# The relation products of a pair in one run at the head of an iteration

## The chip, the cores and the metric

The kernel runs on one core of a Trainium2 chip. The metric is the device time of one execution in microseconds (us). TensorE is called PE, VectorE DVE, ScalarE ACT, GpSimd POOL and SyncE SP, as in the profile.

## The reference

A graph of 6250 nodes with 256 features and 100000 edges passes through two layers, each a graph step and a feed-forward step with a layer norm ahead and a residual sum behind. Cut to the part in which the change lies:

```python
# layer 0, graph: attention over the incoming edges of each node, 8 heads of 32
e = leaky_relu(a_src[src] + a_dst[dst], 0.2)
alpha = softmax of e over the edges with one dst
x = x + relu(segment_sum(h[src] * alpha, dst) + bias)
# layer 0, feed-forward: one of 32 experts for each node, 64 hidden units
xf = layernorm(x)
idx = argmax(xf @ router_w.T + router_b)
x = x + relu(relu(xf @ W1[idx] + b1[idx]) @ W2[idx] + b2[idx])
# layer 1, graph: 16 relations
transformed = einsum('ni,rio->rno', layernorm(x), weight)
x = x + segment_sum(transformed[edge_type, src] * edge_weight, dst)
# layer 1, feed-forward: 8 experts mixed by two weights, not touched here
```

## The kernel before, in words

The nodes are sorted by their number of incoming edges, most first, and stand in 49 tiles of 128. After a preparation (to about 360 us) the function `attention` computes the attention, the first feed-forward step and `transformed` in one software pipeline (to about 2240 us). `relations` then gathers rows of `transformed`, and the last feed-forward step ends the kernel.

`attention` works on pairs of tiles, g = 0 to 23, and a last single tile, g = 24. Each engine runs its own in-order program, a loop over `pair`, and waits on semaphores of the others. The stages of a pair are spread over several iterations:

- POOL (`tile`, L819) gathers for each edge slot of a tile one row of `h_table` per node, 32 columns at most. A tile's first 16 columns may come once the tile two before it is summed, the others once the tile before it is summed.
- DVE (`tile`) scores the gathered rows (L1201 to L1206), looks up the next indices (L1209 to L1218), waits for ACT's exponential (semaphore `p_ready`), weighs (L1231) and adds (L1240) the rows slot by slot, a tile of high degree having more slots, sums (L1254, L1255) and normalises (L1298 to L1307). In the first tile of pair i, between scores and weighing, stands `lagged(i)`: `finish(i - 3)` adds the experts' result (L1155, waits for PE's L1027), `varied` tells ACT that the variances are there, `choose(i - 2)` takes the router's best expert (L1136 to L1144), `norms(i)` normalises (L1174, L1180).
- ACT (`pair(i)`): the exponential of the first tile (`exps`, L860), the roots of the variances (`roots`, L873, waits for `varied`, with a table load ahead of it and one behind it at L874), the copies of the relation products of pair i - 4 (`chunk`, L910), among them `one_hot(i - 2)` (L890, L891), the ReLUs of the hidden units (`relus`, L901, eight for a pair), the exponential of the second tile behind the fourth of these, and two copies of transposed tiles (L881).
- PE (`pair(g)`): the relation products of pair g - 2 (`chunk`, L1037, 16 for a pair, each 128 nodes by 512 outputs), the transposes of the one-hot choice (`one_turn`, L985), eight steps into the hidden units (`into`, L1004 and L998) and eight steps out of them (`outof`, L1022, the last with L1027), the transposes of two other pairs (L959) and the router (`route`, L975). Products go to two PSUM banks in turn, so the third of a run waits for ACT's copy of the first.
- SP stores each copied product (L773) in order. ACT copies into four buffers in turn, so a copy waits for the store of the product four before.

PE's `pair(g)` and ACT's `pair(g + 2)` go together. How the 16 products of a pair are placed among the experts' steps is set by two numbers, `EARLY_T, LATE_T` (L604), which both programs read: products 0 to `EARLY_T` - 1 stand ahead of `one_turn`, product `EARLY_T` behind it, one product behind each step k while `EARLY_T + 1 + k < LATE_T`, two behind the last `into`, and the rest behind the last `outof`. On ACT the rest stands behind the first of the two L881 copies.

Of the kernel before, what the change touches and what calls it, by code (L numbers as in the profile page):

```python
# [584 lines left out]
def attention(p: Program):  # L585
# [15 lines left out]
    CW = 2 * D  # L601
    SLOTS_T = 4
    ahead = AHEAD
    EARLY_T, LATE_T = 5, 12  # L604
    with p.phase() as ctx:
        def sb(n, s, d):
            return ctx.enter_context(nc.sbuf_tensor(n, s, d))
# [1243 lines left out]
def build(nc, a):  # L1851
    with ExitStack() as ctx:
        p = Program(nc, ctx, a)
        search_and_project(p)
        attention(p)
        p.rec = p.keep("rec", [P, NT, D], F32)
        relations(p)
        choose_two(p)
        feed_forward(p)
# [33 lines left out]
```

How the kernel before makes its waits and increments, by code:

```python
    def __call__(self, ins, alone=False):  # L82
        ins.then_inc(self.sem, 1)
        self.n += 1
        self.eng.wait_ge(self.sem, self.base + self.n)
        if alone:
            self.p.alone(self.eng)
# [88 lines left out]
    def moments(self, dve, chain, row=None):  # L176
        ms = self.p.ms
        if row is not None:
            moments(self.p, dve, chain, self.stats, range(NT), row).then_inc(self.varied, 1)
        dve.wait_ge(self.rooted, 1)
        chain(dve.reciprocal(ms[:, :, 3], ms[:, :, 2]))
# [1 line left out]
    def root(self, act, known=False):  # L184
        ms = self.p.ms
        if not known:
            act.wait_ge(self.varied, 1)
        act.activation(ms[:, :, 2], ms[:, :, 1], ACT.Sqrt, bias=self.p.eps[:, 0:1]).then_inc(self.rooted, 1)
# [1 line left out]
    def norm(self, dve, x, g, u):  # L190
        ms = self.p.ms
        dve.wait_ge(self.turned, done(g - U))
        dve.tensor_scalar(self.xn[u][:], x, ms[:, bass.ds(g, 1), 0:1].rearrange("q o c -> q (o c)"),
                          ms[:, bass.ds(g, 1), 3:4].rearrange("q o c -> q (o c)"),
                          ALU.subtract, ALU.mult).then_inc(self.normed, 1)
# [1 line left out]
    def turn(self, pe, g, u):  # L197
        pe.wait_ge(self.normed, done(g))
        pe.wait_ge(self.copied, done(g - 3))
        for k in range(KD):
            ins = pe.transpose(self.p.bank[u % 4][:, k * P:(k + 1) * P], self.xn[u][:, k * P:(k + 1) * P], self.p.ident[:])
        ins.then_inc(self.turned, 1)
# [150 lines left out]
        @block.gpsimd  # L353
# [23 lines left out]
            pool.wait_ge(edge_in, 48)  # L377
            pool.wait_ge(key_ready, 1)
```

## Time and profile before

| | us |
|---|---|
| median of 3 runs | 3732.01 (3728.25 to 3733.63) |
| the profiled execution | 3733.77 |
| its span, from the first to the last instruction | 3732.0 |
| busy in the span: PE | 2049.4 |
| busy in the span: DVE | 1761.7 |
| busy in the span: POOL | 1966.1 |
| busy in the span: ACT | 799.2 |

Times of the trace count from the start of the span. A row of the timeline merges neighbouring instructions of one kind; "x8" is their count, and a number in brackets is the time for which the engine had been idle before, with what ended it. A matrix product of this kernel, in 32-bit floats, shows as two records for each instruction of the program, so a relation product (two instructions) is four records of L1037.

### The profile page before, as it was taken

The page shows a single profiled execution, that of the slowest core. Times are in us where ns is not written, and L with a number is a line of the kernel's source. Part 1 is how long each engine was busy: PE and PEld are TensorE (multiplying, and loading weights), DVE is VectorE, ACT ScalarE, POOL GpSimd, SP SyncE. Part 2 cuts the span into 40 slices and gives each one's busy share as a digit, 9 for nine tenths or more (in the row PEclk, how much of TensorE's full clock was granted, in tenths as well). Part 3 has the DMA queues.
Part 4 walks back from the last instruction along what each step waited for, and adds up shares of the span by engine and source line. Part 5 has one row for each costly group of instructions (what it writes and reads, how often), then busy time and mean ns, then how long its engine had stood idle before and what let it go on. Part 6 is the DMA issues. An engine that isn't in the chain of part 4 may idle for free. (4 is left out here: it accounts for less than half of the span.)

```text
span 3732.0 us, 38147 instructions
## 1 busy us (share of the span) xinstructions
PE 2049.4 (55%) x7510; PEld 1300.8 (35%) x7510; DVE 1761.7 (47%) x3926; ACT 799.2 (21%) x1653; POOL 1966.1 (53%) x1919
## 2 busy tenths in 40 slices
PE   1600025799999999999999930000000000069996
PEld 1400024466565656566665510000000000056664
DVE  6632646566665555554441024444444444314445
ACT  3300001233333333333333310000000000013331
POOL 5444888888675554444310047777777776400111
PEclk9855567899999999999999965555555555569998
DMA  6636233555555454444422253333333333200000
GB/s 234 219 86 180 78 87 86 148 156 148 159 145 155 136 149 131 142 131 124 127 89 79 83 177 105 105 105 105 105 104 105 105 104 91 69 29 9 20 17 24
DMA packets 209083, 415.27 MB, mean 111 GB/s; under 512 B 53563, under 2 KB 96019, under 8 KB 208931
## 3 DMA queue, kind: packets, MB, share of 16 engines
q0 software_dynamic: 87168, 239.28, 23.8%
q1 hardware_dynamic: 114706, 167.99, 12.9%
q10 hardware_dynamic: 7056, 6.63, 0.5%
q14 instruction: 137, 1.11, 0.1%
q8 instruction: 16, 0.26, 0.0%
HBM read 259.06 MB, written 154.68 MB: 111 GB/s over the span
## 5 line engine op out<-in xcount | busy, mean ns | idle before, releaser
L819 POOL DMA_INDIRECT gat_rows<-h_table,gat_idx x824 | 942.9, 1144 | 580.3 <-DVE gat_acc L1255 337.0
L1378 POOL DMA_INDIRECT rel_rows<-transformed,rel_idx x824 | 779.0, 945 | 549.1 <-issue 538.4
L1037 PE MATMUL bank<-tr_wr,tr_xt 128*128 128x512 f32 x1568 | 727.5, 601 | 43.9 <-ACT tr_row L910 39.0
L1536 PE MATMUL bank<-weight,rec 128*128 128x1 f32 x196 | 42.0, 352 | 1083.1 <-DVE weight L1562 1083.1
L1446 DVE SCALAR_TENSOR_TENSOR bank<-rel_rows,rel_weight,bank 128x256 f32<-128x256 f32 x775 | 379.1, 489 | 213.9 <-DMA rel_rows<-transformed,rel_idx 75.2
L1004 PE MATMUL bank<-mo_xt,mo_w 128*128 128x256 f32 (+1 forms) x1600 | 432.7, 394 | 21.9 <-ACT mo_ht L901 20.3
L1536 PEld LDWEIGHTS bank<-weight,rec 128*128 128x128 f32 x196 | 41.9, 333 | 1083.9 <-DVE weight L1562 1083.9
L1037 PEld LDWEIGHTS bank<-tr_wr,tr_xt 128*128 128x128 f32 x1568 | 291.2, 191 | 339.3 <-issue 267.1
L910 ACT ACTIVATE tr_row<-bank 128x512 f32<-128x512 f32 x392 | 231.4, 596 | 657.8 <-PE bank L1037 657.8
L1022 PE MATMUL bank<-mo_w,mo_ht 128*128 128x256 f32 x1568 | 366.9, 379 | 0.0
L1004 PEld LDWEIGHTS bank<-mo_xt,mo_w 128*128 128x128 f32 x1600 | 287.6, 193 | 155.1 <-issue 97.0
L1231 DVE TENSOR_TENSOR gat_rows<-gat_rows 128x1024 f32<-128x1024 f32 (+1 forms) x169 | 254.3, 1528 | 148.8 <-ACT gat_rows L860 148.8
L1022 PEld LDWEIGHTS bank<-mo_w,mo_ht 128*128 128x128 f32 x1568 | 297.8, 190 | 50.2 <-issue 11.0
L1418 ACT ACTIVATE rel_idx<-rel_key_i 128x2 int32 (+1 forms) x265 | 54.1, 204 | 1005.9 <-DMA rel_rows<-transformed,rel_idx 1005.9
L901 ACT ACTIVATE mo_ht<-bank,mo_b 128x256 f32<-128x256 f32 (+1 forms) x400 | 165.9, 466 | 353.4 <-PE bank L1004 317.5
L1750 POOL DMA_INDIRECT out<-ff_z,ff_at x49 | 48.8, 996 | 360.5 <-DVE ff_z L1830 349.6
L1240 DVE TENSOR_TENSOR gat_rows<-gat_rows 128x1056 f32<-128x1056 f32 x169 | 211.8, 1253 | 7.2
L1444 DVE TENSOR_SCALAR bank<-rel_rows,rel_weight 128x256 f32<-128x256 f32 x49 | 23.9, 487 | 331.6 <-DMA rel_rows<-transformed,rel_idx 311.3
L1684 PE MATMUL bank<-ff_xt,ff_w 128*128 128x512 f32 (+1 forms) x416 | 173.5, 575 | 7.0 <-ACT ff_xt L1720 7.0
L1693 PE MATMUL bank<-ff_w,ff_gt 128*128 128x256 f32 x784 | 171.3, 379 | 0.0
L1693 PEld LDWEIGHTS bank<-ff_w,ff_gt 128*128 128x128 f32 x784 | 148.8, 190 | 25.1 <-issue 5.3
L1155 DVE SCALAR_TENSOR_TENSOR tr_x<-bank,tr_x 128x256 f32 (+1 forms) x49 | 18.6, 420 | 206.3 <-PE bank L1027 205.6
(261 smaller groups left out, 1991.2 us busy)
## 6 DMA issues: line engine op xcount, KB each, us to landing
transformed<-tr_row SPq DMA_DIRECT2D x392, 256.0 KB, 2.1
windows<-win SPq DMA_DIRECT2D x34, 736.0 KB, 3.2
gat_rows<-h_table,gat_idx POOLq DMA_INDIRECT x824
rel_rows<-transformed,rel_idx POOLq DMA_INDIRECT x824, 2.7
h_table<-hrow ACTq DMA_DIRECT2D x49, 132.0 KB, 2.3
xa<-x SPq DMA_DIRECT2D x1, 6272.0 KB, 23.8
rec<-x_moved SPq DMA_DIRECT2D x1, 6272.0 KB
tr_x<-records SPq DMA_DIRECT2D x24, 256.0 KB, 3.5
```

The lines of the kernel that those rows point to most:

```text
L819: pool.indirect_dma_start(out=rows[:, column(u, j), :], out_offset=None, in_=p.h_table[:], in_offset=bass.IndirectOffsetOnAxis(ap=idx[u][: ...
L901: ins = act.activation(ht[:, b % HALF, 0:n * P], p.bank[2 + k % 2][:, h * PT:h * PT + n * P], ACT.Relu, bias=b1[:, b:b + 1])
L910: act.activation(trow[c % SLOTS_T][:], p.bank[6 + c % 2][:], ACT.Copy).then_inc(evacuated, 1)
L1004: ins = pe.matmul(to[h], w1[:, kd, b * P:(b + 1) * P], xt[:, kd, 0:n * P], start=(h == 0 and kd == 0), stop=(h == 1 and kd == KD - 1))
L1022: ins = pe.matmul(p.bank[4 + u][:, 0:D], ht[:, b % HALF, u * P:(u + 1) * P], w2[:, b, :], start=(b == 0), stop=False)
L1037: ins = pe.matmul(p.bank[6 + c % 2][:], xt2[:, k, u * P:(u + 1) * P], wr[:, k, m * CW:(m + 1) * CW], start=(k == 0), stop=(k == KD - 1))
L1231: dve.tensor_tensor(m[:, :, :, 0:HEAD_DIM], m[:, :, :, 0:HEAD_DIM], m[:, :, :, HEAD_DIM:HW].broadcast_to([P, COLS[s], HEADS, HEAD_DIM]), A ...
L1240: dve.tensor_tensor(total, total, columns(u, JCOL, 2 * JCOL) if s == 0 else part(s), ALU.add).then_inc(added[s], 1)
L1378: pool.indirect_dma_start(out=rows[s][:, j, :], out_offset=None, in_=p.transformed[:], in_offset=bass.IndirectOffsetOnAxis(ap=idx[s][:, j: ...
L1446: ins = dve.scalar_tensor_tensor(total, rows[s][:, j, :], w(j), total, ALU.mult, ALU.add)
L1684: ins = pe.matmul(p.bank[2 + ef % 4][:, 0:tiles * P], w1[:, ef // F, k, (ef % F) * P:(ef % F + 1) * P], xt[slot][:, k, 0:tiles * P], start ...
L1693: ins = pe.matmul(p.bank[6 + j % 2][:, 0:D], gt[slot][:, ef, j * P:(j + 1) * P], w2[:, ef, :], start=(ef == 0), stop=(ef == EF - 1))
```

## The change

Two numbers are changed, in the line that both programs read:

```diff
-    EARLY_T, LATE_T = 5, 12
+    EARLY_T, LATE_T = 15, 16
```

With 15 and 16, products 0 to 14 of a pair stand ahead of `one_turn`, product 15 behind it, and none is left for the steps of the experts or behind them. This holds for PE and ACT alike; SP's order follows the products' numbers and stays.

PE, the head of the loop's body. L1037 is a relation product (two rows for each), L985 the one-hot transposes, L1004 and L998 a step into the hidden units, L1022 a step out of them. Before:

```order
L1037 MATMUL bank<-tr_wr,tr_xt 128x512 x10
L985 MATMUL bank<-mo_identb,mo_hot 32x128 x2
L1037 MATMUL bank<-tr_wr,tr_xt 128x512 x2
L1004 MATMUL bank<-mo_xt,mo_w 128x256 x2
L998 MATMUL bank<-mo_nots,mo_other 128x256 x2
L1004 MATMUL bank<-mo_xt,mo_w 128x256 x2
L1037 MATMUL bank<-tr_wr,tr_xt 128x512 x2
L1004 MATMUL bank<-mo_xt,mo_w 128x256 x2
L998 MATMUL bank<-mo_nots,mo_other 128x256 x2
L1004 MATMUL bank<-mo_xt,mo_w 128x256 x2
L1037 MATMUL bank<-tr_wr,tr_xt 128x512 x2
```

Now, with the changed numbers:

```order
L1037 MATMUL bank<-tr_wr,tr_xt 128x512 x30
L985 MATMUL bank<-mo_identb,mo_hot 32x128 x2
L1037 MATMUL bank<-tr_wr,tr_xt 128x512 x2
L1004 MATMUL bank<-mo_xt,mo_w 128x256 x2
L998 MATMUL bank<-mo_nots,mo_other 128x256 x2
L1004 MATMUL bank<-mo_xt,mo_w 128x256 x4
L998 MATMUL bank<-mo_nots,mo_other 128x256 x2
L1004 MATMUL bank<-mo_xt,mo_w 128x256 x4
L998 MATMUL bank<-mo_nots,mo_other 128x256 x2
L1004 MATMUL bank<-mo_xt,mo_w 128x256 x2
L1022 MATMUL bank<-mo_w,mo_ht 128x256 x4
```

Fifteen products stand ahead of L985 where five stood, and the experts' steps follow one another without a product between them.

ACT, from the end of the roots to the exponential of the second tile (L860), in the first iteration that has products; the loop's body has the same order. L910 copies a relation product, L901 is a ReLU of hidden units (two rows for each step), L890 and L891 belong to the one-hot choice. Before, its last rows up to the exponential:

```order
L901 ACTIVATE mo_ht<-bank,mo_b 128x256 x2
L910 ACTIVATE tr_row<-bank 128x512
L901 ACTIVATE mo_ht<-bank,mo_b 128x256 x2
L910 ACTIVATE tr_row<-bank 128x512
L901 ACTIVATE mo_ht<-bank,mo_b 128x256 x2
L910 ACTIVATE tr_row<-bank 128x512
L689 TENSOR_LOAD items
L689 ISA x2
L860 ACTIVATE gat_rows<-gat_score 128x32x8
```

Now:

```order
L910 ACTIVATE tr_row<-bank 128x512 x15
L890 ACTIVATE mo_nots<-bank 32x256
L891 ACTIVATE mo_ones<-bank 32x256
L910 ACTIVATE tr_row<-bank 128x512
L901 ACTIVATE mo_ht<-bank,mo_b 128x256 x8
L689 TENSOR_LOAD items
L689 ISA x2
L860 ACTIVATE gat_rows<-gat_score 128x32x8
```

The exponential stands behind 16 copies and four ReLU steps, where it stood behind ten copies and four ReLU steps.

## Rows read from the trace of the kernel before

**Rows 1.** Busy time by stretch: us, then each engine's busy us (count), PEclk, DMA, GB/s
```profile
1100.00:2000.00 900.00, 885.44 (x3230) 547.00 (x3229) 468.26 (x998) 307.33 (x589) 388.53 (x388) 1.00 0.44 129
```

**Rows 2.** Waits of PE, 700 to 2100 us: total, times, longest
```profile
PE bank L1037 <- ACT tr_row L910: 20.6, 20, 2.2
```

**Rows 3.** Timeline of PE, one iteration: start, us, engine, line, operation
```profile
1446.48 3.70 PE L1037 MATMUL bank<-tr_wr,tr_xt 128*128 128x512 f32 x8
1451.11 5.42 PE L1037 MATMUL bank<-tr_wr,tr_xt 128*128 128x512 f32 x12 [0.93 <-ACT tr_row L910]
1456.45 0.29 PE L985 MATMUL bank<-mo_identb,mo_hot 128*32 128x128 bf16 x2
...
1458.49 1.03 PE L1004 MATMUL bank<-mo_xt,mo_w 128*128 128x256 f32 x4
...
1491.84 1.89 PE L1022 MATMUL bank<-mo_w,mo_ht 128*128 128x256 f32 x8
1493.57 1.03 PE L1004 MATMUL bank<-mo_xt,mo_w 128*128 128x256 f32 x4
...
1495.81 1.89 PE L1022 MATMUL bank<-mo_w,mo_ht 128*128 128x256 f32 x8
...
1510.66 3.70 PE L1037 MATMUL bank<-tr_wr,tr_xt 128*128 128x512 f32 x8
```

**Rows 4.** Waits of DVE, 700 to 2100 us
```profile
DVE gat_rows L1231 <- ACT gat_rows L860: 147.9, 20, 10.9
```

**Rows 5.** Timeline of DVE in the same iteration
```profile
1479.69 3.43 DVE L1231 TENSOR_TENSOR gat_rows<-gat_rows 128x2048 f32<-128x2048 f32 x2 [8.13 <-ACT gat_rows L860]
...
1489.08 0.43 DVE L1255 TENSOR_TENSOR gat_acc<-gat_rows 128x264 f32<-128x264 f32 x1
...
1498.04 0.62 DVE L1201 TENSOR_TENSOR gat_score<-gat_rows,info 128x256 f32<-128x256 f32 x1 [0.26 <-DVE gat_mask L1196]
...
1506.05 0.76 DVE L1155 SCALAR_TENSOR_TENSOR tr_x<-bank,tr_x 128x256 f32 x2 [3.65 <-PE bank L1027]
```

**Rows 6.** Timeline of PE, a run of products at the stage's end
```profile
2139.63 22.48 PE L1037 MATMUL bank<-tr_wr,tr_xt 128*128 128x512 f32 x52
```

**Rows 7.** Timeline of ACT in the iteration of rows 3
```profile
1447.46 1.28 ACT L873 ACT_TABLE_LOAD   x1
...
1461.03 0.84 ACT L901 ACTIVATE mo_ht<-bank,mo_b 128x256 f32<-128x256 f32 x2 [1.63 <-PE bank L1004]
...
1478.88 0.67 ACT L860 ACTIVATE gat_rows<-gat_score 128x256 f32<-128x256 f32 x1 [0.18 <-issue]
```

**Rows 8.** Timeline of PE, the third product of three early iterations
```profile
675.31 7.08 PE L1037 MATMUL bank<-tr_wr,tr_xt 128*128 128x512 f32 x12 [18.40 <-ACT tr_row L910]
...
742.46 7.11 PE L1037 MATMUL bank<-tr_wr,tr_xt 128*128 128x512 f32 x12 [2.23 <-ACT tr_row L910]
...
809.34 5.42 PE L1037 MATMUL bank<-tr_wr,tr_xt 128*128 128x512 f32 x12 [1.94 <-ACT tr_row L910]
```

**Rows 9.** Timeline of DVE, the finish ahead of the product at 742.46
```profile
736.50 0.76 DVE L1155 SCALAR_TENSOR_TENSOR tr_x<-bank,tr_x 128x256 f32 x2 [0.28 <-issue]
```

**Rows 10.** Busy time of L1231 in three weighings of second tiles: us, DVE busy (count)
```profile
1094.00:1107.00 13.00, 5.88 (x4) 1.00 0.41 115
1158.00:1170.00 12.00, 4.65 (x3) 1.00 0.30 85
...
1735.00:1746.00 11.00, 3.43 (x2) 1.00 0.13 48
```

**Rows 11.** The page's costliest groups: the additions of DVE, count, busy, mean ns
```profile
L1240 DVE TENSOR_TENSOR gat_rows<-gat_rows 128x1056 f32<-128x1056 f32 x169 | 211.8, 1253 | 7.2
```

**Rows 12.** Busy time by stretch around the product at 742.46, columns of rows 1
```profile
740.00:743.00 3.00, 0.77 (x3) 0.31 (x3) 2.08 (x10) 2.85 (x6) 2.39 (x3) 1.00 0.91 315
743.60:746.90 3.30, 3.30 (x5) 1.24 (x5) 3.30 (x3) 0.60 (x1) 3.16 (x1) 0.50 0.61 198
```

**Rows 13.** The page's DMA issues: the stores of the products, KB, us to landing
```profile
transformed<-tr_row SPq DMA_DIRECT2D x392, 256.0 KB, 2.1
```

## The prediction

> **What bounds the kernel now.** The change touches one stage, from about 360 to 2240 us, in which all engines work on node tiles two at a time. I read the busy time by stretch first: from 1100 to 2000 us TensorE (PE) is busy 885 of 900 us at a granted clock of 1.00, its upper level of 2.4 GHz, while DVE has 468, ACT 307 and POOL 389 [rows 1]. So PE sets the pace, and its waits come next: between 700 and 2100 us it waits 20 times, 20.6 us in all, each time in front of a relation product and for ACT's copy of an earlier one [rows 2]. The timeline of PE shows one iteration, which I call a lap. It starts at 1446.48 with two products, the third is late, at 1451.11, and the next lap starts at 1510.66 [rows 3]: 64.18 us. Undisturbed the third product would start at about 1449.93 (1.72 us a product), so 1.2 us of a lap are lost and PE's own work is 63.0 us. There is therefore little to gain here (20 laps, 24 us); the question is whether something that now hides in the 63 us comes out.
>
> What hides there is a loop through three engines. DVE weighs the rows of the pair's second tile only after ACT's exponential (L860), which stands in ACT's queue behind the copies of ten products and four ReLUs; DVE waits 147.9 us for it in 20 laps [rows 4], 8.13 us in the lap shown [rows 5]. Then DVE sums, normalises, scores the first tile of the next pair and finishes an older pair (L1155); only after that may ACT take its roots (L873), which stand ahead of the next lap's first copy, which PE's third product needs.
>
> **What moves.** No instruction is added or dropped. The ten products that stood behind the one-hot transposes (L985) and the experts' steps now stand ahead of them; the sixteenth stays just behind L985. ACT's copies and SP's stores follow the same order. The new place of the exponential follows from that. I measure everything from PE's resumption, the start of the third product.
>
> To the weighing of the second tile, after the change: 13 products in a run take 22.48 us [rows 6] (52 records of four to a product); L985 and the sixteenth product 2.04 us (1456.45 to 1458.49); four steps into the hidden units at 2.24 us (1493.57 to 1495.81), and one step out of them at 1.73 us (1491.84 to 1493.57) [rows 3]. That is 35.2 us. ACT's fourth ReLU starts 0.30 us after the step (1458.49 + 2.24 = 1460.73 to 1461.03) and takes 0.84; the exponential starts about 0.3 later (0.18 is the row's gap; a load of the tile's count may add to it), and DVE 0.81 after its start (1478.88 to 1479.69) [rows 5, 7]. Sum 37.5 us. Before it is 1479.69 - 1451.11 = 28.6. **The second tile is weighed 8.9 us later.**
>
> How much of that is slack? DVE waits 3.65 us for the experts' result (L1027) before it finishes the older pair [rows 5]. From the start of that finish to PE's resumption it takes 5.96 us where nothing else is late (736.50 to 742.46) [rows 8, 9], but 9.2 us in the usual lap (1506.05 to 1510.66 + 4.63), because ACT then still has an exponential of the first tile and, behind it, the table load at 1447.46 [rows 7]: another 3.3 us. Together 6.9 us, or 6.6 with the hand-off that stays. 8.9 less 6.6 leaves 2.2 us that come out.
>
> The same as a whole lap: 37.5 to the weighing; 9.8 to the end of the sum (1479.69 to 1489.51); 8.5 to the first score operation of the next tile (1498.04); 4.6 to the finish (1506.05 - 3.65 - 1498.04 = 4.4, and 0.28 to hand over); 5.96 to the resumption. **66.4 us, against 64.18.** That holds for a second tile of three slots. A slot costs DVE one weighing (1.2 us: 5.88 for four, 4.65 for three) and one addition (1.25) more or less, 2.4 together [rows 10, 11]. With four slots the lap is 68.8, with two it would be 64.0. There a floor takes over, the experts' result. The finish that waits for it starts 4.61 us ahead of the next lap (1506.05, 1510.66); two products that stood between, 3.44, go to the head, which leaves 1.17, and the resumption is 5.96 after it, 4.8 us into the lap instead of 4.63. So 64.4.
>
> The slots of the second tiles are read from the weighings: four in the laps that start with the resumptions from 675 to 1066 us, three from 1130, two from 1708 on [rows 10]. That makes 7, 9 and 4 laps.
> - Four slots: before, 67.15 and 66.88 us for the first two (675.31, 742.46, 809.34) [rows 8] and five of 64.18, 454.9 in all. After: 7 x 68.8 = 481.6. **+26.7.** Here POOL gathers nearly without a pause before, so part of these tiles' data may be late as well; the gathers of a first tile beyond 16 columns wait for the second tile's sum, and two to four gathers plus landing fit in the 8.5 us. I put nothing for it, and up to +10 into the range.
> - Three slots: 9 x (66.4 - 64.18) = **+20.0.**
> - Two slots: 4 x 0.2 = **+0.8.** The two or three laps after the last tile start without that stall before; by the floor they now wait about 1.3 each: **+2.6.**
>
> **The clock.** A stall costs more than its length. After the wait of 2.23 us at 742 the granted clock was 0.50 (1.2 GHz) from 743.6 to 746.9; after the wait of 1.94 us at 809 twelve records took 5.42 us, not 7.11, and with the waits of 0.93 us it stayed at 1.00 [rows 1, 8, 12]. Some 3.4 us at half clock cost 1.7 us of PE time, and they lie in the loop, ahead of the exponential, so nothing absorbs them. The four-slot laps will stall 68.8 - 63.0 = 5.8 us: all 7 pay, **+11.9.** The three-slot laps stall 3.4 us, 3.1 as the trace counts it, above the only length that was seen to cost; but one row is thin evidence, so I take two in three: 9 x 1.7 x 2/3 = **+10.2.** The bounds are 0 and 15.3. The Trainium skill ("TensorE: Matmul & The Clock Gate", the section on why this matters) warns against long idle gaps between bursts of matmuls, as they send the clock back to half rate; by that rule the five-microsecond stalls pay and shorter ones might not, which would take the 10.2 us away; the row at 743 speaks for paying already at 2.23.
>
> The 5.96 us to the resumption contain two loads of ACT's tables. The Trainium skill ("ScalarE: Activation LUTs", "What ACT_TABLE_LOAD costs") puts a switch at about 2.66 us with its drain, an estimate of 2.8 us more for the two than their rows show. This trace has 1.28 us each, with the next instruction right behind, so nothing is added.
>
> **Sum.** 26.7 + 20.0 + 0.8 + 2.6 + 11.9 + 10.2 = 72 us. The profiled execution took 3733.8 us (span 3732.0) against a median of 3732.0, so the difference can be set on the median: **3804 us**, 1.9% slower.
>
> **Rivals.**
> 1. *The delay stays hidden* (7%). It decides at 6.6 us: if the exponential came no more than that later, by products that run faster in a row or a shorter path on DVE, no three-slot lap would grow. For it speaks only DVE's large idle share; against it that each link above is a measured one. It gives 3732, or 3735 to 3755 if the four-slot laps alone grow.
> 2. *Faster* (3%): the stall at the head goes, if sixteen products in a row let PE run over ACT's late start. Two PSUM banks (6 and 7) allow two products ahead, at the head as before, so I see no way; it would give 3732 - 20 x 1.2 = 3708.
> 3. *The stores become the limit* (5%): sixteen stores of 256 KB every 1.72 us are 153 GB/s, beside gathers. ACT has four buffers, so a store may take some 6 us from its copy; it lands in 2.1 [rows 13]. If the pitch in the run rose to 2.2 us, 14 products would lose 7 us in each of 22 laps: 3730 + 72 + 150, about 3950. Against it speaks that the queues moved 315 GB/s at times (740 to 743 us) [rows 12]. The Trainium skill ("DMA: Bandwidth & Descriptors", "Specifications") gives some 358 GB/s as one core's limit at the memory; stores and gathers together would stay below it.
> 4. *The clock is worse than taken* (7%): a stall of 5.8 us may leave PE at half clock for about twice 3.4 us, or the growing lap meets late gathers as well: 3835 to 3860.
> 5. *My forecast* (78%): the loop through ACT and DVE sets the lap; without any loss to the clock it gives 3782, with all laps paying 3809, and an error of 1 us in a lap moves it by 16.
>
> That the change doesn't do what it says can be left out: the rows of the order show the run of 15 and the sixteenth product.
>
> **The range** for 8 in 10 is 3768 to 3834: the forecast's own bounds, 3782 less 14 and 3809 plus 25. A measurement of this kernel can tell about 0.2%, 7.5 us. Slower by more than that: the forecast, rivals 3 and 4, and two points of rival 1, 0.92 in all; within it 0.05; faster 0.03.
>
> **What would show each step.** After the change PE's wait before L1037 should be some 3 us in laps of three slots, 5 to 6 in laps of four, and about 1.2 in laps of two, with laps of 66.4 to 68, 68.8 to 70.5 and 64.4 us. DVE's wait for L860 should grow from about 8 to about 17 us, and its wait before L1155 vanish in laps of three and four slots. The clock's record should dip to 0.5 right after most stalls. ACT's table load at L873 should wait for DVE rather than stand behind the exponential. If laps of three slots stay at 64.2, the chain is wrong; if the products of the head run lie further apart than 1.72 us, it is the stores.

## The result and the profile after

| | before | after |
|---|---|---|
| median us (4 runs each) | 3732.78 (3728.25 to 3733.63) | 3808.38 (3806.95 to 3809.34) |
| span of the profiled execution, us | 3732.0 | 3806.2 |
| ratio of the runs, 95% interval | | 1.0205 (1.0187 to 1.0222) |

The change costs 75.6 us. The forecast was 3804 us, slower, with a range of 3768 to 3834.

The waits of PE from 700 to 2170 us, in total, times and longest, answer to [rows 2] (the stretch is 70 us longer, as the stage is):

```profile
PE bank L1037 <- ACT tr_row L910: 70.8, 22, 5.4
PE bank L1037 <- ACT tr_xt L881: 0.4, 1, 0.4
```

and the waits of DVE in the same stretch to [rows 4]:

```profile
DVE gat_rows L1231 <- ACT gat_rows L860: 333.0, 20, 18.7
DVE tr_x L1155 <- PE bank L1027: 114.4, 6, 57.7
```

PE still waits only ahead of relation products, but for 70.8 us instead of 20.6. DVE's wait for the exponential of the second tile has grown from 147.9 to 333.0 us in 20 laps again. Its wait for the experts' result, 3.65 us in the lap of [rows 5], is left in 6 places only, 57.7 us of it in one.

The timeline of PE in one lap of three slots, as [rows 3]. A lap is one iteration of the loop, counted here from PE's third product to the next lap's; its slots are those of the pair's second tile. The columns are start, us, engine, line, operation, and in brackets the idle time before:

```profile
1502.58 3.69 PE L1037 MATMUL bank<-tr_wr,tr_xt 128*128 128x512 f32 x8
1509.26 22.58 PE L1037 MATMUL bank<-tr_wr,tr_xt 128*128 128x512 f32 x52 [2.99 <-ACT tr_row L910]
1531.78 0.29 PE L985 MATMUL bank<-mo_identb,mo_hot 128*32 128x128 bf16 x2
1531.99 1.98 PE L1037 MATMUL bank<-tr_wr,tr_xt 128*128 128x512 f32 x4
1533.82 1.03 PE L1004 MATMUL bank<-mo_xt,mo_w 128*128 128x256 f32 x4
...
1544.52 1.89 PE L1022 MATMUL bank<-mo_w,mo_ht 128*128 128x256 f32 x8
...
1568.69 3.70 PE L1037 MATMUL bank<-tr_wr,tr_xt 128*128 128x512 f32 x8
```

The fourth step into the hidden units ends about where L1022 starts, at 1544.52. The timelines of ACT and of DVE in that lap, as [rows 7] and [rows 5]:

```profile
1502.94 0.68 ACT L860 ACTIVATE gat_rows<-gat_score 128x256 f32<-128x256 f32 x1 [0.51 <-issue]
1505.61 1.28 ACT L873 ACT_TABLE_LOAD   x1 [2.00 <-DVEq L1187]
...
1507.23 1.28 ACT L874 ACT_TABLE_LOAD   x1
...
1508.63 1.07 ACT L910 ACTIVATE tr_row<-bank 128x512 f32<-128x512 f32 x2
...
1544.81 0.84 ACT L901 ACTIVATE mo_ht<-bank,mo_b 128x256 f32<-128x256 f32 x2 [3.13 <-PE bank L1004]
1545.61 0.67 ACT L860 ACTIVATE gat_rows<-gat_score 128x256 f32<-128x256 f32 x1
```

```profile
1546.43 3.43 DVE L1231 TENSOR_TENSOR gat_rows<-gat_rows 128x2048 f32<-128x2048 f32 x2 [15.91 <-ACT gat_rows L860]
...
1555.82 0.43 DVE L1255 TENSOR_TENSOR gat_acc<-gat_rows 128x264 f32<-128x264 f32 x1
...
1564.78 0.62 DVE L1201 TENSOR_TENSOR gat_score<-gat_rows,info 128x256 f32<-128x256 f32 x1 [0.26 <-DVE gat_mask L1196]
1569.42 0.76 DVE L1155 SCALAR_TENSOR_TENSOR tr_x<-bank,tr_x 128x256 f32 x2 [0.28 <-issue]
```

From PE's resumption at 1509.26 to the weighing at 1546.43 are 37.2 us (forecast 37.5, before 28.6). The finish at 1569.42 no longer waits for PE, and ACT's table load at 1505.61, which in the kernel before started as soon as the exponential ahead of it had ended, now waits 2.00 us for DVE. That is the loop of the prediction, closed.

Where the time went, by PE's third product at the bounds of the lap classes. The rows of after:

```profile
675.23 8.98 PE L1037 MATMUL bank<-tr_wr,tr_xt 128*128 128x512 f32 x17 [16.96 <-ACT tr_row L910]
...
1170.33 2.07 PE L1037 MATMUL bank<-tr_wr,tr_xt 128*128 128x512 f32 x2 [5.36 <-ACT tr_row L910]
...
1778.82 3.70 PE L1037 MATMUL bank<-tr_wr,tr_xt 128*128 128x512 f32 x8 [2.98 <-ACT tr_row L910]
...
2035.88 4.56 PE L1037 MATMUL bank<-tr_wr,tr_xt 128*128 128x512 f32 x10 [0.94 <-ACT tr_row L910]
...
2237.16 14.00 PE L1037 MATMUL bank<-tr_wr,tr_xt 128*128 128x512 f32 x32 [0.86 <-ACT tr_xt L881]
```

and those of before, beside 675.31 in [rows 8]:

```profile
1130.23 4.13 PE L1037 MATMUL bank<-tr_wr,tr_xt 128*128 128x512 f32 x9 [0.92 <-ACT tr_row L910]
...
1707.81 4.56 PE L1037 MATMUL bank<-tr_wr,tr_xt 128*128 128x512 f32 x10 [0.94 <-ACT tr_row L910]
...
1964.20 5.42 PE L1037 MATMUL bank<-tr_wr,tr_xt 128*128 128x512 f32 x12 [0.62 <-ACT tr_row L910]
...
2163.18 14.00 PE L1037 MATMUL bank<-tr_wr,tr_xt 128*128 128x512 f32 x32 [0.86 <-ACT tr_xt L881]
```

| stretch | before | after | more | forecast |
|---|---|---|---|---|
| 7 laps of four slots | 454.9 | 495.1 | 40.2 | 38.6 |
| 9 laps of three slots | 577.6 | 608.5 | 30.9 | 30.2 |
| 4 laps of two slots | 256.4 | 257.1 | 0.7 | 0.8 |
| the rest of the stage | 199.0 | 201.3 | 2.3 | 2.6 |

The whole stage is 74.0 us later at its last products, and the span is 74.2 us longer. A lap's cost to the clock comes after its stall, so that of the stall at 1170.33 lies in the first lap of three slots.

### The profile page after: what moved, and what is told of

Read it like the earlier page. It is cut to its first block and busy times, and to the rows that moved or that the text cites. A ratio compares the mean times of both kernels' runs of the same rounds, so it can differ in the third digit from the quotient of the medians.

```text
span 3806.2 us, 38147 instructions
## 1 busy us (share of the span) xinstructions
PE 2073.4 (54%) x7510; PEld 1310.0 (34%) x7510; DVE 1761.4 (46%) x3926; ACT 800.9 (21%) x1653; POOL 1916.1 (50%) x1919
## 5 line engine op out<-in xcount | busy, mean ns | idle before, releaser
L819 POOL DMA_INDIRECT gat_rows<-h_table,gat_idx x824 | 894.7, 1086 | 700.0 <-DVE gat_acc L1255 459.4
L1037 PE MATMUL bank<-tr_wr,tr_xt 128*128 128x512 f32 x1568 | 721.5, 617 | 91.3 <-ACT tr_row L910 88.1
L1037 PEld LDWEIGHTS bank<-tr_wr,tr_xt 128*128 128x128 f32 x1568 | 302.8, 197 | 475.6 <-issue 362.5
L1004 PE MATMUL bank<-mo_xt,mo_w 128*128 128x256 f32 (+1 forms) x1600 | 425.2, 394 | 22.4 <-ACT mo_ht L901 20.8
L1231 DVE TENSOR_TENSOR gat_rows<-gat_rows 128x1024 f32<-128x1024 f32 (+1 forms) x169 | 254.1, 1527 | 333.9 <-ACT gat_rows L860 333.9
L1022 PE MATMUL bank<-mo_w,mo_ht 128*128 128x256 f32 x1568 | 364.0, 380 | 0.0
L1004 PEld LDWEIGHTS bank<-mo_xt,mo_w 128*128 128x128 f32 x1600 | 287.2, 193 | 105.7 <-issue 51.9
L910 ACT ACTIVATE tr_row<-bank 128x512 f32<-128x512 f32 x392 | 231.0, 596 | 427.2 <-PE bank L1037 427.2
L1022 PEld LDWEIGHTS bank<-mo_w,mo_ht 128*128 128x128 f32 x1568 | 298.5, 191 | 40.7
L901 ACT ACTIVATE mo_ht<-bank,mo_b 128x256 f32<-128x256 f32 (+1 forms) x400 | 165.9, 466 | 485.7 <-PE bank L1004 397.8
L1684 PEld LDWEIGHTS bank<-ff_xt,ff_w 128*128 128x128 f32 x416 | 76.4, 192 | 97.4 <-issue 95.1
```

The costliest lines, as they stand in the source:

```text
L819: pool.indirect_dma_start(out=rows[:, column(u, j), :], out_offset=None, in_=p.h_table[:], in_offset=bass.IndirectOffsetOnAxis(ap=idx[u][: ...
L901: ins = act.activation(ht[:, b % HALF, 0:n * P], p.bank[2 + k % 2][:, h * PT:h * PT + n * P], ACT.Relu, bias=b1[:, b:b + 1])
L910: act.activation(trow[c % SLOTS_T][:], p.bank[6 + c % 2][:], ACT.Copy).then_inc(evacuated, 1)
L1004: ins = pe.matmul(to[h], w1[:, kd, b * P:(b + 1) * P], xt[:, kd, 0:n * P], start=(h == 0 and kd == 0), stop=(h == 1 and kd == KD - 1))
L1022: ins = pe.matmul(p.bank[4 + u][:, 0:D], ht[:, b % HALF, u * P:(u + 1) * P], w2[:, b, :], start=(b == 0), stop=False)
L1037: ins = pe.matmul(p.bank[6 + c % 2][:], xt2[:, k, u * P:(u + 1) * P], wr[:, k, m * CW:(m + 1) * CW], start=(k == 0), stop=(k == KD - 1))
```

## The experiments

Each kernel is either the one before or the changed one with a small edit in ACT's or PE's program. The theory: what costs is the later place of the second tile's exponential, in a loop that runs over DVE and ACT's roots back to PE's third product. The rival: the run of sixteen products costs by itself, through stores, copies or the clock.

### The exponential moved ahead of the ReLUs, the run kept

```diff
--- the changed kernel
                 chunk(i - 4, EARLY_T)
+                if width(i) == 2:
+                    exps(i, 1, 2 * i + 1)
                 for k in range(BANKS):
                     relus(i - 2, k)
                     if EARLY_T + 1 + k < LATE_T:
                         chunk(i - 4, EARLY_T + 1 + k)
-                    if k == BANKS // 2 - 1 and width(i) == 2:
-                        exps(i, 1, 2 * i + 1)
```

> The changed kernel with one thing moved: ACT's exponential of the second tile stands right behind the sixteenth copy, ahead of the ReLUs, where it stood behind the fourth ReLU. PE's order, the run of sixteen products and the stores stay as in the changed kernel. My theory (the loss is the later exponential, through DVE and the roots back to PE's third product): the exponential can start about 25.3 us after PE's resumption, 11 earlier than after the change and 2.5 earlier than before it, so the chain is shorter than PE's work in all laps, the laps are set by the floor (the finish that waits for the experts' result) at 64.35 us, no dip of the clock after 760 us, and the time is 3732.8 + 20 x 0.17 + 2.6 = 3739 us. Rival A (the run of sixteen products itself costs, by stores, copies or the clock): nothing is regained, 3800 to 3810. Rival B (it is the order of PE around the experts): also 3800 or more.

Measured: 3734.3 us, ratio to before 1.0010 (1.0001 to 1.0020). One operation moved on ACT gives back practically all of the loss, with the run of sixteen products in place. PE's lap and DVE's finish in this kernel:

```profile
1443.47 3.70 PE L1037 MATMUL bank<-tr_wr,tr_xt 128*128 128x512 f32 x8
1448.38 22.59 PE L1037 MATMUL bank<-tr_wr,tr_xt 128*128 128x512 f32 x52 [1.21 <-ACT tr_row L910]
...
1507.80 3.70 PE L1037 MATMUL bank<-tr_wr,tr_xt 128*128 128x512 f32 x8
```

```profile
1475.24 3.43 DVE L1231 TENSOR_TENSOR gat_rows<-gat_rows 128x2048 f32<-128x2048 f32 x2 [5.60 <-ACT gat_rows L860]
...
1506.75 0.76 DVE L1155 SCALAR_TENSOR_TENSOR tr_x<-bank,tr_x 128x256 f32 x2 [8.67 <-PE bank L1027]
```

The run takes 22.59 us for 13 products, as at the stage's end before [rows 6], and the lap is 64.33 us, the floor that was worked out as 64.35. It came out 4.7 us under the expectation because the first two laps of four slots became shorter than before too (64.3 us against 67.15 and 66.88 [rows 8], of which 1.7 each are the clock's). There the exponential was already in a loop in the kernel before, by a way that the prediction doesn't sum: DVE waited 1.21 us for it, the gathers of the next tile wait for the second tile's sum, and DVE then waited for their rows, so that its finish [rows 9] had no wait for PE left:

```profile
731.90 0.62 DVE L1201 TENSOR_TENSOR gat_score<-gat_rows,info 128x256 f32<-128x256 f32 x1 [6.05 <-DMA gat_rows<-h_table,gat_idx]
```

With the exponential earlier this wait is 4.54 us, and the finish waits 2.37 us for PE. That the gathers are the link is read from the program and these waits; no run tests it alone.

### The exponential moved back, the products left where they were

```diff
--- the kernel before
-                    if k == BANKS // 2 - 1 and width(i) == 2:
+                    if k == 5 and width(i) == 2:
                         exps(i, 1, 2 * i + 1)
```

> The kernel before with one thing moved: ACT's exponential of the second tile stands behind the sixth ReLU step instead of the fourth. PE's order and the spread of the products stay as before. It then starts two steps of 5.69 us later, 11.4 us, against 8.9 in the changed kernel. My theory: with a slack of 6.6 us at three slots, laps grow by 4.8 us at three slots, 7.2 at four, 2.4 at two: 9 x 4.8 + 7 x 7.2 + 4 x 2.4 = 103 us, and 16 to 20 laps with a dip of the clock at 1.7 to 2.4 us add 27 to 45: 3863 to 3881 us, with no product moved at all. Rival A (the run of products costs): no change, 3733 us. Rival C (the delay counts, but only beside the missing cover of the products): something under 3780.

Measured: 3886.4 us, ratio 1.0418 (1.0400 to 1.0435). Without any product moved the kernel is twice as much slower as by the change. PE's waits, 700 to 2250 us, and one lap of three slots:

```profile
PE bank L1037 <- ACT tr_row L910: 130.0, 20, 8.7
```

```profile
1552.18 7.75 PE L1037 MATMUL bank<-tr_wr,tr_xt 128*128 128x512 f32 x12 [6.10 <-ACT tr_row L910]
...
1623.86 2.07 PE L1037 MATMUL bank<-tr_wr,tr_xt 128*128 128x512 f32 x2 [6.10 <-ACT tr_row L910]
```

The lap is 71.7 us, 7.5 over the 64.18 of before. The clock is paid behind 19 of the 20 stalls here (the last one is 0.62 us): the three products behind the stall shown take 7.75 us instead of 5.42, 2.3 more. The delay itself is 11.8 us, not 11.4 (the transposes L959, 0.44, stand in between as well), which with the slack of 6.6 gives 5.2: 64.2 + 5.2 + 2.3 = 71.7. The time is 5 us above the expectation's upper end, and 0.4 us in each of 20 laps are 8.

The same with the fifth ReLU step instead of the sixth (`if k == 4`):

> The kernel before with the exponential of the second tile behind the fifth ReLU step: 5.7 us later than before, below the slack of 6.6 us that I worked out for laps of three slots and above the 4.2 of laps of four. Theory: laps of three and two slots stay at 64.18; laps of four slots grow by 1.5 us each, 10 us, some of them with a dip of the clock, up to 12 more: 3743 to 3755 us. If there were no slack, 5.7 us in 20 laps would give 114 us more, 3847 us.

Measured: 3757.3 us, ratio 1.0069 (1.0052 to 1.0086). Laps of three and two slots stayed at 64.18 us, but for the first of three, which has the clock's cost of the stall ahead of it. The stalls at the ends of the seven laps of four are 3.2 to 3.5 us, and after six of them the clock dipped; five of these laps take 68.0 to 68.3 us, one without a dip 66.5, and the first, behind a stall of 21 us, 69.5. One of the five, PE and DVE:

```profile
1016.75 7.11 PE L1037 MATMUL bank<-tr_wr,tr_xt 128*128 128x512 f32 x12 [3.33 <-ACT tr_row L910]
...
1085.02 7.11 PE L1037 MATMUL bank<-tr_wr,tr_xt 128*128 128x512 f32 x12 [3.33 <-ACT tr_row L910]
```

```profile
1053.16 3.43 DVE L1231 TENSOR_TENSOR gat_rows<-gat_rows 128x2048 f32<-128x2048 f32 x2 [13.07 <-ACT gat_rows L860]
```

Resumption to weighing is 36.4 us, of which 1.7 are the clock's (7.11 for three products against 5.42); 34.7 - 28.6 = 6.1 us of delay, again 0.4 more than I had counted. A lap of three slots has the same delay (34.72 us from resumption to weighing) and keeps its length:

```profile
1411.66 5.42 PE L1037 MATMUL bank<-tr_wr,tr_xt 128*128 128x512 f32 x12 [0.93 <-ACT tr_row L910]
...
1475.84 5.42 PE L1037 MATMUL bank<-tr_wr,tr_xt 128*128 128x512 f32 x12 [0.93 <-ACT tr_row L910]
```

```profile
1446.38 3.43 DVE L1231 TENSOR_TENSOR gat_rows<-gat_rows 128x2048 f32<-128x2048 f32 x2 [14.15 <-ACT gat_rows L860]
```

So a delay of 6.1 us is free where the slack is 6.6, and costs where it is 4.2. The time is 2 us above the range expected; 0.4 us in each of seven laps are 2.8.

### A run of fourteen

```diff
-    EARLY_T, LATE_T = 5, 12
+    EARLY_T, LATE_T = 13, 14
```

> The two numbers at 13 and 14: thirteen products ahead of the one-hot transposes, one behind, two behind the last step into the hidden units. The exponential stands behind 14 copies, two products (3.44 us) less than in the change. Theory: three slots 66.4 - 3.4 = 63.0, which is under the floor of 64.35, so 64.35; four slots 68.8 - 3.4 = 65.4, with stalls of about 2.4 us that may or may not dip the clock. Sum: 7 x 1.2 + 13 x 0.17 + 2.6 = 13 us, plus 0 to 12 for the clock: 3746 to 3758 us. Rival A (cost in proportion to the length of the run): 9/11 of 76 us, 3795 us.

Measured: 3742.7 us, ratio 1.0030 (1.0019 to 1.0041). With 8 of the ten products moved ahead of L985 (the expectation's 9 of 11 is a miscount), 14% of the loss is there. A cost in proportion to the run would have given about 3793. The laps of three and two slots are 64.33 us (the floor), but for the first, which pays a dip; six of those of four are 65.0 to 65.4, with stalls of 1.7 to 2.2 us. Only one of the seven stalls, of 2.0 us, was followed by a dip. So the loss has a threshold, and in laps of three slots only the last two products cross it.

### The clock's share

Three matrix instructions whose result nobody reads (each half a relation product, 0.86 us) fill a part of the stall:

```diff
--- the changed kernel, PE
+                    if c == 2:
+                        for _ in range(3):
+                            pe.matmul(p.bank[0][:], xt2[:, 0, 0:P], wr[:, 0, 0:CW], start=True, stop=True)
                     at_least(pe, evacuated, g * 2 * CHUNKS_T + c - 1)
```

> The changed kernel with three idle instructions added on PE ahead of the third product of each pair: products of 128x512 into a PSUM bank that is free at that point, whose result nobody reads. They take 3 x 0.86 = 2.6 us at full clock and lie inside the stall (3.0 us in laps of three slots, 5.3 in laps of four). It measures the clock's share. Theory: laps of three slots are never short of work on PE for 2 us, so the six dips of the clock in them vanish, 6 x 1.7 = 10 us; laps of four slots keep a gap of some 2.7 us and may keep their dips (7 laps at about 2.4 to 3.4 us). The laps of two slots have a stall of 1.2 us and become 1.4 us longer, 4 to 6 of them, +7. Sum 3808 - 10 + 7 = 3805 us, or down to 3788 if the dips of the four-slot laps go too; the laps of three slots all at 66.1 us. If the clock had no part in the loss, those laps would stay a mixture of 66.1 and 67.8 us.

This kernel and the next three ran first on a chip on which PE, ACT and DVE stood still together for some 10 us at a time, while POOL went on with its gathers: the kernel before took 4380.8 us there (the disturbed chip below). The kernel before with the table's reload moved (below) shows one such pause (POOL, then ACT):

```profile
1255.05 0.94 POOL L819 DMA_INDIRECT gat_rows<-h_table,gat_idx  x1 [0.30 <-issue]
```

```profile
1260.54 1.08 ACT L914 ACTIVATE tr_row<-bank 128x512 f32<-128x512 f32 x2 [10.57 <-remote]
```

The filled kernel gave 4571.6 us there, ratio 1.0426 (1.0384 to 1.0468), which tells little of a 20 us effect. All four were run again on other chips.

> The same kernel as e5_fill (the changed kernel with three idle products ahead of each pair's third), whose runs stood on the chip on which the engines paused together. The expectation is unchanged: no dip of the clock in laps of three slots, all of them at 66.1 us, six dips of 1.7 us gone; two-slot laps 1.4 us longer; 3805 us, or down to 3788 if the dips of the four-slot laps go too. If the clock had no part, the three-slot laps stay a mixture of 66.1 and 67.8 us.

Measured: 3804.7 us, ratio 1.0195 (1.0178 to 1.0212), an interval that overlaps the changed kernel's, so the total time does not show the clock's share; the laps and the clock's record do. The stretch from 1200 to 1780 us lies in the laps of three slots; first the changed kernel, then this one (us, then each engine's busy us, granted clock, DMA share, GB/s):

```profile
1200.00:1780.00 580.00, 552.31 (x2007) 342.61 (x2006) 305.84 (x640) 189.54 (x362) 267.61 (x268) 0.98 0.43 128
```

```profile
1200.00:1780.00 580.00, 575.31 (x2075) 352.90 (x2074) 316.45 (x655) 192.69 (x366) 270.31 (x271) 1.00 0.44 130
```

With the stall filled the clock stays at 1.00 in laps of three slots, and eight of the nine take 66.1 to 66.3 us (the first, 67.5, pays the dip of the last four-slot stall). In the changed kernel two of the nine are 66.1, six 67.8 to 68.0, each of the six with one dip to 0.50 right after the stall at its head, and the first is 69.2, behind a four-slot stall:

```profile
1306.20:1309.50 3.30, 3.30 (x6) 1.24 (x5) 3.30 (x4) 0.50 (x1) 2.78 (x2) 0.50 0.85 224
```

So the part of the clock behind three-slot stalls is 6 x 1.7 = 10 us. In laps of four slots 2.7 us of idle time stayed, and the dips as well; the laps of two slots grew to 65.4 us, as the added 2.6 us are longer than their stall of 1.2.

### The table's reload behind the second copy

```diff
                     act.activation(mom[:, lo:hi, 2], mom[:, lo:hi, 1], ACT.Sqrt, bias=p.eps[:, 0:1]).then_inc(rooted, 1)
-                    act.activation(warm[:], p.eps[:], ACT.Exp)
+            def rewarm(i):
+                lo, hi = (0 if width(i - 1) else 2), (2 + width(i - 3) if width(i - 3) else width(i - 1))
+                if lo < hi:
+                    act.activation(warm[:], p.eps[:], ACT.Exp)
...
-                for c in range(EARLY_T):
+                for c in range(2):
+                    chunk(i - 4, c)
+                rewarm(i)
+                for c in range(2, EARLY_T):
                     chunk(i - 4, c)
```

In the changed kernel it shortens the loop by 1.5 us and nothing else:

> The changed kernel with the table's reload behind the second copy and nothing else. It shortens the loop from the exponential back to PE by 1.5 us. Theory: laps of three slots 66.1 - 1.5 = 64.6, with stalls under 2 us and hardly a dip; four slots 68.5 - 1.5 = 67.0 plus 1.7 to 2.4 for the clock; two slots at PE's own 62.9. Sum against before: 7 x 67.0 - 454.9 = +14, clock +12 to +17, 9 x 0.4 = +4, 4 x -1.3 = -5: 3757 to 3762 us. If the loop did not pass through ACT's roots, the time would stay at 3808 less at most a few.

On the disturbed chip 4507.7 us, ratio 1.0283 (1.0241 to 1.0325). Again:

> The same kernel as e8_after_warm (the changed kernel with the table's reload behind the second copy), for the same reason. The expectation is unchanged: laps of three slots 64.6 us, of four 67.0 plus 1.7 to 2.4 for the clock, of two 62.9; 3757 to 3762 us. If the loop did not pass through ACT's roots, 3808 less at most a few.

Measured: 3758.1 us, ratio 1.0067 (1.0050 to 1.0084), 50 us less than the change. Its waits of PE, 700 to 2100 us, and a lap of three slots:

```profile
PE bank L1044 <- ACT tr_row L914: 40.2, 16, 3.9
```

```profile
1475.24 3.70 PE L1044 MATMUL bank<-tr_wr,tr_xt 128*128 128x512 f32 x8
1480.43 22.58 PE L1044 MATMUL bank<-tr_wr,tr_xt 128*128 128x512 f32 x52 [1.49 <-ACT tr_row L914]
...
1539.86 3.69 PE L1044 MATMUL bank<-tr_wr,tr_xt 128*128 128x512 f32 x8
```

The lap is 64.6 us, the 66.1 less 1.5 that was expected, and no three-slot stall is followed by a dip. What ACT does between DVE's finish and the first copy is in the loop.

In the kernel before, the same edit attacks the stall of 1.2 us at the head of each lap:

> The kernel before with one thing moved: the small exponential that loads ACT's table back after the roots (L874, 1.28 us of load and 0.2) stands behind the copies of the first two products instead of ahead of them. The first copy then ends some 3.2 us into the lap instead of 4.6, and PE's third product finds it done. Theory: the stall of 1.2 us at the head of 20 laps goes and laps are PE's own 62.9 us: 3732 - 20 x 1.3 = 3706 us. Rival: PE's head waits for something else as well (DVE's roots and the choice of the expert), and the laps stay above 63.5 us, 3718 us or more.

On the disturbed chip 4373.6 us, ratio 0.9986 (0.9964 to 1.0008). Again:

> The same kernel as e6_warm, whose four runs stood on a chip on which all engines paused together several times in each lap (the kernel before took 4381 us there against 3732), so that differences of 20 us could not be read. The expectation is unchanged: the stall of 1.2 us at the head of 20 laps goes, laps of 62.9 us, 3706 us in all; above 3718 if PE's head waits for something else too.

Measured: 3706.8 us, ratio 0.9932 (0.9919 to 0.9946); the kernel before took 3729.8 us on that chip. And both edits on the run of sixteen (the exponential ahead of the ReLUs, the reload behind the second copy):

> The changed kernel (run of sixteen) with both moves: the exponential of the second tile ahead of the ReLUs, and the table's reload behind the second copy. Theory: the floor of 64.33 us that the finish sets is made of 1.17 ahead of the lap, 5.96 to the resumption; the reload takes 1.5 out of it, so the resumption could come 3.3 us into the lap, when PE gets there by itself (3.43): laps of 62.9 to 63.1 us, 3704 to 3710 us, the same as the other order with the reload moved. Rival (the run of sixteen products itself costs): it stays above that one by more than 0.3%.

On the disturbed chip 4472.6 us, ratio 1.0203 (1.0162 to 1.0243). Again:

> The same kernel as e7_run_early_warm, for the same reason. The expectation is unchanged: the run of sixteen products with the exponential ahead of the ReLUs and the table's reload behind the second copy, laps of 62.9 to 63.1 us, 3704 to 3710 us, like the other order with the reload moved. If the run itself costs, it stays above that by more than 0.3%.

Measured: 3705.7 us, ratio 0.9938 (0.9924 to 0.9951). PE's waits from 700 to 2100 us, first with the order of before, then with the run of sixteen:

```profile
PE bank L1044 <- ACT tr_row L914: 2.2, 2, 1.8
PE bank L1044 <- ACT tr_xt L885: 0.5, 1, 0.5
```

```profile
PE bank L1011 <- ACT mo_ht L905: 2.2, 1, 2.2
PE bank L1044 <- ACT tr_row L914: 1.1, 1, 1.1
PE bank L1044 <- ACT tr_xt L885: 0.4, 1, 0.4
```

PE's waits are nearly gone in both, their usual laps are 62.98 and 62.86 us, and the two kernels agree within their intervals. Both beat the kernel before and the changed one. The run of sixteen products is neither dear nor cheap in itself; what it moves on ACT decides.

## Why the prediction was right

- *What bounds the stage.* PE's own work of a lap, forecast at 63.0 us, is 62.86 to 62.98 where nothing stalls it. The 1.2 us at the head of a lap were ACT's, and could be had: 24 us forecast as the most for 20 laps, and with the reload moved the stage's last products come 25.3 us earlier (2137.86 against 2163.18).
- *The delay of the exponential.* 37.2 us after the resumption against 37.5 forecast, 8.6 later than before instead of 8.9; the products of the run keep their pitch.
- *The slack of 6.6 us.* It holds: at three slots a delay of 6.1 us costs nothing, one of 8.6 makes a lap of 66.1 us (66.4 forecast), one of 11.8 a lap of 69.4 before the clock.
- *Slots.* The classes of 7, 9 and 4 laps behaved as three cases, and the floor of 64.4 for two slots came out at 64.33.
- *The clock behind three-slot stalls.* Two in three were taken to pay, and six of the nine stalls did; the filled stall shows it to be the clock. The chance for a stall near the edge came from one row, so that it hit exactly is luck.
- *Terms that were mis-sized.* Both loops were put a little too long and the clock too cheap. Without the clock the laps of four slots are 68.4 us (68.8 forecast) and those of three 66.1 (66.4), together 5 us less than forecast. The seven dips behind four-slot stalls cost 1.5 to 3.0 us each, 2.6 on the mean and not 1.7 (from the dips' lengths and the products' times), as six of them last 6.8 us and not 3.4. The last falls into the laps of three slots, where the clock took some 13 us and not 10.2. With the dip of the first lap, which the kernel before has too, the clock took about 29 us, 22.1 forecast. The errors cancel but for about 2 us, and that is luck too.
- *The gathers.* For these the range held 10 us. In laps of four slots DVE still waits for gathered rows, 3.49 us at 767.37, but then 13.00 us for the exponential, so that they cost nothing that shows.
- *Rivals.* A hidden delay (1) fell by the traces; a head without stall (2) by 70.8 us of waits; stores as the limit (3) by the run's pitch of 22.58 us for 13 products and by the kernel with the exponential moved, though the median landing of a store did rise from 2.1 to 2.8 us (2.3 with the exponential moved). Rival 4, the clock worse than taken, was half right: six of the seven dips behind four-slot stalls did last twice 3.4 us, but a part of each lies in the stall itself, and what they cost stays far from its 3835 us.

## What to carry to other kernels

When a change moves work in a queue, look for the one instruction behind it for which another engine waits, and follow that engine until it comes back to the first; sum the loop from measured rows, and take off the waits in it, which are its slack. An engine that is busy half the time can still be the one whose lateness costs. Where the slack ends the loss starts at once. A stall of the matrix engine can cost more than its length, through the clock behind it: in these traces some of the stalls from 2.0 us on did, and all from 3.75 us on.

## What the runs showed of the hardware

- A stall of PE is followed by half clock in a way that its length alone does not decide. Stalls ahead of a lap's third product between 700 and 2100 us, as counted in the traces of undisturbed chips: 0.9 to 1.6 us, never; 1.7 to 2.2 us, 2 of 10 (the kernel before, the run of fourteen, the early reload; 2.23 paid, 2.21 and 2.14 did not, one of 2.0 did); 3.0 to 3.5 us, 12 of 16 (the change, the exponential behind the fifth ReLU); from 3.75 us on, all (7 of the early reload on the changed kernel, 7 of the change, 19 of the exponential behind the sixth ReLU). The dips last 3.4 us (behind the three-slot stalls of the change), 6.8 (behind six of its four-slot stalls) or 10.2 (behind five stalls of 8.3 to 8.7 us, the exponential behind the sixth ReLU).
- With three unread matrix instructions in the stall, a remaining gap of 2.6 to 2.7 us was followed by a dip in all seven laps, and one of 0.4 to 0.6 us in none of nine. Without them six of nine stalls of 3.0 to 3.1 us were.
- One chip ran every kernel 17% or more slower, with pauses of PE, ACT and DVE of some 10 us in which POOL went on. The order of products mattered more there: the changed order with both moves was 2.0% behind the kernel before, and 0.6% ahead elsewhere. Why the engines paused, and why this order lost more by it, is open.
